# One edge group of the second layer summed in the input projection, and the sum tables zeroed in the first stage

## What is computed

```python
h = relu(layernorm(x)) @ w_in + b_in            # the input projection
for l in range(2):                              # two attention layers
    xn = layernorm(h, ln1_g[l], ln1_b[l])
    q, k, v = xn @ wq[l] + bq[l], xn @ wk[l] + bk[l], xn @ wv[l] + bv[l]
    scores = (q[dst] * k[src]).sum(-1) * scale          # per head, 8 heads
    attn = segment_softmax(scores, dst)
    agg = segment_sum(attn[:, :, None] * v[src], dst)
    h = h + agg @ wo[l] + bo[l]
    h = h + gelu(layernorm(h, ln2_g[l], ln2_b[l]) @ w1[l] + b1[l]) @ w2[l] + b2[l]
x = x + h
h = relu(layernorm(x))
sum3d = segment_sum(edge_attr @ W_sum + b_sum, src)     # needs nothing of the attention layers
x = x + h + z_in[in_deg] + z_out[out_deg] + sigmoid(cent @ W_cent + b_cent) + sigmoid(vor @ W_vor + b_vor) + sum3d
```

## Time and profile before

| | us |
|---|---|
| median of 3 runs | 4973.2 |
| lowest and highest run | 4970.74, 4974.58 |
| span of the profiled execution | 4968.2 |
| PE busy | 3781.3 (76%) |
| DVE busy | 3674.6 (74%) |
| POOL busy | 3293.4 (66%) |
| ACT busy | 2245.8 (45%) |
| costliest line: scatters of the updates, POOL L1523, x600 | 951.8 |

### The profile page before, as it was taken

The page is one execution under the profiler, slowest core; times in us unless marked ns, Lnnn a source line. Parts: engine busy times, 40 slices in busy tenths (PEclk is TensorE's granted clock), DMA queues, the critical chain, the costliest instruction groups (busy, mean ns, idle before and its releaser), DMA issues. The chain is left out here.

```text
span 4968.2 us, 83663 instructions
## 1 busy us (share of the span) xinstructions
PE 3781.3 (76%) x17490; PEld 2898.5 (58%) x17491; DVE 3674.6 (74%) x10004; ACT 2245.8 (45%) x5559; POOL 3293.4 (66%) x2856
## 2 busy tenths in 40 slices
PE   2686677777777776999986677777777776888879
PEld 1344455555555555888853455555555555777766
DVE  5686688888888886666656688888888886666658
ACT  0122455555555553444410455555555563343323
POOL 2266666666666654888877666666666663888866
PEclk9698799988988998999998799999899997999989
DMA  4577666666666655777766666666666654777767
GB/s 107 176 173 172 195 184 180 184 181 180 185 175 184 178 159 127 152 160 153 160 133 132 199 181 187 183 181 181 180 180 181 183 172 97 148 143 148 143 157 222
DMA packets 683884, 831.82 MB, mean 167 GB/s; under 512 B 147301, under 2 KB 524321, under 8 KB 683589
## 3 DMA queue, kind: packets, MB, share of 16 engines
q0 software_dynamic: 261248, 480.06, 40.8%
q1 hardware_dynamic: 389483, 320.59, 22.4%
q10 hardware_dynamic: 32860, 28.05, 1.9%
HBM read 753.81 MB, written 124.16 MB: 177 GB/s over the span
## 5 line engine op out<-in xcount | busy, mean ns | idle before, releaser
L1042 POOL DMA_INDIRECT kv<-kv_scratch,src_u x1760 | 1775.7, 1009 | 955.1 <-issue 532.4
L1308 PE MATMUL sum_p<-msg,hot_s 128*128 128x273 f32 x3520 | 1132.7, 460 | 578.9 <-DVE sums L1174 452.6
L1308 PEld LDWEIGHTS sum_p<-msg,hot_s 128*128 128x128 f32 x3520 | 705.2, 215 | 893.1 <-DVE sums L1174 442.8
L1523 POOL DMA_INDIRECT sum_scratch<-ysum,dest x600 | 951.8, 1586 | 196.8 <-issue 137.8
L1296 PE MATMUL qe<-sums,hot_q 128*128 x3520 | 910.0, 404 | 99.6 <-ACT hot_q L1064 85.7
L1296 PEld LDWEIGHTS qe<-sums,hot_q 128*128 128x128 f32 x3520 | 719.5, 208 | 244.7 <-issue 115.7
L1174 DVE SCALAR_TENSOR_TENSOR sums<-sums,keep,sum_p 128x273 f32 x880 | 433.7, 493 | 463.9 <-remote 402.1
L1073 ACT ACTIVATE hot_s<-iota_f,ndrel_u 128x128 f32<-128x128 f32 x1760 | 558.7, 391 | 223.1 <-remote 173.2
L1148 DVE TENSOR_TENSOR prod<-qe,kv 128x1024 f32<-128x1024 f32 x440 | 535.6, 1217 | 64.2 <-DMA kv<-kv_scratch,src_u 35.0
L1163 DVE TENSOR_TENSOR msg<-kv,turned 128x1024 f32<-128x1024 f32 x440 | 532.6, 1210 | 7.5 <-issue 7.5
L1155 DVE TENSOR_REDUCE S<-prod 128x32 f32<-128x1024 f32 x440 | 533.8, 1213 | 0.6
(11 more groups left out here) (267 smaller groups left out, 5147.8 us busy)
## 6 DMA issues: line engine op xcount, KB each, us to landing
drow<-drel_scratch SPq DMA_DIRECT2D x220, 256.0 KB
kv<-kv_scratch,src_u POOLq DMA_INDIRECT x1760
ea<-in_edge_attr SPq DMA_DIRECT2D x52, 512.0 KB
srow<-in_src_rows SPq DMA_DIRECT2D x52, 512.0 KB
kv_scratch<-res SPq DMA_DIRECT2D x100, 256.0 KB
ea<-in_edge_attr SPq DMA_DIRECT2D x52, 384.0 KB
srow<-in_src_rows SPq DMA_DIRECT2D x52, 384.0 KB
h_scratch<-res SPq DMA_DIRECT2D x150, 128.0 KB
```

What stands on the lines that cost most here:

```text
L1042: g.indirect_dma_start(out=kv[:, slot, :], out_offset=None, in_=KVd, in_offset=bass.IndirectOffsetOnAxis(ap=src_u[:, par, u:u + 1], axis=0 ...
L1308: ins = pe.matmul(sum_p[i][:, 0:XW], hot_s[:, q % 2, 2 * i + u, :], msg[:, q % 2, 2 * i + u, :], start=(u == 0), stop=(u == 1))
L1523: g.indirect_dma_start(out=sum_d[r], out_offset=bass.IndirectOffsetOnAxis(ap=dest[:, k, j:j + 1], axis=0), in_=ysum[:, k, j, :], in_offset ...
```

## The change

It has two parts.

**One more group early.** `OPENING = ((1, 5),)` names layer 1 (the second), group 5. `project(-1)` now handles that group for each of the 50 tiles: two groups a pair (`EN` = 2, `halves` = 1), so one `y_p`, tables 0 and 1 only, one `ysum` copy and two scatters a pair. `OWN = (6, 5)` says how many groups the updates scatter themselves: the second update now has 5 groups a tile, in two parts of 3 and 2, and scatter `j` of tile `k` goes to table `(5k + j) mod 4`. The waits on the four table semaphores in `project(0)` start from the count that `project(-1)` leaves (`scattered(r)`). In `project(-1)` POOL's list gets scales and scatters in turn (`first_turn`), DVE's the compare, the count and the destination of the group, SP's the three loads, and its wait at the end is for the landing of the scatters.

**Zeroing.** The four tables are zeroed in the first stage, on ACT's queue, by 10 stores for each table (semaphore `tables_out`, which POOL waits for before its first scatter), from a tile of zeros `zero`. The 100 stores in `project(-1)` are gone.

```diff
+OWN = (6, 5)
+OPENING = ((1, 5),)
+ZERO_PARTS = 10
+ZERO_W = NT * YW // ZERO_PARTS
...
+                @block.scalar
+                def _(a):
+                    a.wait_ge(zeroed, 1)
+                    for r in range(TABLES):
+                        table = sum_d[r].rearrange("(p a) w -> p (a w)", p=P)
+                        for i in range(ZERO_PARTS):
+                            a.dma_start(table[:, i * ZERO_W:(i + 1) * ZERO_W], zero[:, 0:ZERO_W]).then_inc(tables_out, 16)
...
-            early = l == 0
+            early = l <= 0
+            queries = l == 0
+            EN = 2 * len(OPENING) if first else 2 * HELD
+            halves = EN // 2
...
+                            if first:
+                                for h, (layer, j) in enumerate(OPENING):
+                                    g = layer * NT + t * 2
+                                    sp.dma_start(srow[:, 2 * h * P:(2 * h + 2) * P].rearrange("p (k e) -> p k e", k=2),
+                                                 src_rows[bass.ds(g, 2), j * P:(j + 1) * P].unsqueeze(0).to_broadcast([P, 2, P])
...
-                            if first:
-                                for r in range(TABLES):
-                                    sp.dma_start(sum_d[r][bass.ds(t * 2 * P, 2 * P), :].rearrange("(p a) w -> p (a w)", p=P),
-                                                 sums[:, 0:2 * YW]).then_inc(zero_out, 16)
...
-                        if first:
-                            sp.wait_ge(zero_out, 16 * TABLES * PAIRS)
...
+                        def scale(t, k):
+                            g.wait_ge(ve_s[k], t + 1)
+                            g.tensor_tensor(out=rs[:, k, :], in0=veps[:, k, :], in1=neghalf[:, :],
+                                            op=ALU.pow).then_inc(rs_s[k], 1)
+
+                        def first_turn(t):
+                            scale(t + 1, 1)
+                            if halves == 2 and (not isinstance(t, int) or t > 0):
+                                scatter(t - 1, 1)
+                            scale(t + 2, 0)
+                            scatter(t, 0)
...
+                        if first:
+                            for t, k in ((0, 0), (0, 1), (1, 0)):
+                                scale(t, k)
+                            g.wait_ge(tables_out, 16 * ZERO_PARTS * TABLES)
+                            first_turn(0)
+                            with g.Fori(1, PAIRS) as t:
+                                first_turn(t)
...
                         def early_turn(t):
                             norm(t + 1, 0)
+                            if first:
+                                stats(t + 1, 1)
                             results(t, 0)
...
                             compare(t)
                             norm(t + 1, 1)
+                            if first:
+                                stats(t + 2, 0)
                             results(t, 1)
                             repeats(t)
                             destination(t, 0)
...
-                groups = EG if held is not None else EG - HELD
-                PARTS = ((0, 0, 3), (1, 3, EG - HELD), (0, EG - HELD, EG))[0:3 if held is not None else 2]
+                own_n = OWN[l]
+                groups = own_n + HELD if held is not None else own_n
+                PARTS = ((0, 0, 3), (1, 3, own_n), (0, own_n, own_n + HELD))[0:3 if held is not None else 2]
```

More of the change, by code:

```diff
@@ L500, in wait, with scattered @@
                         eng.wait_ge(sem, v)
+                def scattered(r):
+                    return 0 if first or r >= 2 * len(OPENING) else 16 * PAIRS
                 def scatters_done(eng, t, h):
                     for r in (2 * h, 2 * h + 1):
-                        wait(eng, early_s[r], t * 16)
+                        wait(eng, early_s[r], t * 16 + scattered(r))
                 with nc.Block() as block:
@@ L653, in _ @@
                                             base=0, pattern=[[-1, P]], channel_multiplier=1).then_inc(tril_s, 1)
+                        if first:
[5 more added lines that the diff above has]
+                                first_turn(t)
+                            if halves == 2:
+                                scatter(PAIRS - 1, 1)
+                            for r in range(EN):
+                                g.wait_ge(early_s[r], 16 * PAIRS)
+                        elif early:
                             for h in range(2):
@@ L799, in early_turn @@
                             destination(t, 0)
-                        if not first:
+                        if first:
+                            for k in range(2):
+                                stats(0, k)
+                        else:
                             v.wait_ge(scales_s, 1)
-                            for k in range(2):
-                                norm(0, k)
+                        for k in range(2):
+                            norm(0, k)
+                        if first:
+                            stats(1, 0)
                         if early:
@@ L867, in sum_groups @@
                         def sum_groups(t):
-                            pe.wait_ge(ea_in, t * 32 + 32)
+                            pe.wait_ge(ea_in, (t + 1) * 16 * halves)
                             pe.wait_ge(same_s, t * ES + 2)
-                            for h in range(2):
+                            for h in range(halves):
                                 wait(pe, y_ev[h], t)
@@ L1420, in scatters @@
                     return sum(table(k, j, n) == r for j in range(n))
-                own_n = EG - HELD
                 def part(t, k, b, j0):
                     n = t * 2 + k
-                    return n * 2 + j0 // (EG - HELD) if b == 0 and held is not None else n
+                    return n * 2 + j0 // own_n if b == 0 and held is not None else n
                 per = [[16 * scatters(k, r, own_n) for r in range(TABLES)] for k in range(2)]
-                sc0 = [[l * 16 * scatters(k, r, EG - HELD) * PAIRS for r in range(TABLES)] for k in range(2)]
+                sc0 = [[sum(16 * scatters(k, r, OWN[i]) * PAIRS for i in range(l)) for r in range(TABLES)] for k in range(2)]
                 S3N = groups + 5
@@ L1509, in scatter @@
                             for b, j0, j1 in PARTS:
-                                if held is not None and j0 == EG - HELD:
+                                if held is not None and j0 == own_n:
                                     continue
```

83 lines of the change are left out of this document (38 added, 45 removed).

## The result

The changed kernel takes 4987.1 us in the median of 7 runs (4981.39 to 4995.88), the kernel before 4970.7 us in 7 runs on the same chip. The ratio is 1.0029, with a 95% interval of 1.0017 to 1.0042: slower by 0.29%, a small loss, with 1 outside the interval. The forecast was 4985, slower. The profiled execution of the changed kernel has a span of 4988.5 us against 4968.2. One later execution of the changed kernel, in which the chip granted 0.56 of TensorE's clock instead of 0.90, took 6109 us; it stands in no median and no ratio of this text.

The account below looks back on a forecast made before the run. POOL was taken to bound the second update, a DVE chain the first projection. From 4968.2 us, +73 + 10.7 + 6 + 2 - 79, less about 1, gave 4980; the runs' median being 5.0 above the profile, 4985 us, range 4948 to 5010.

Parts of the forecast that it names:

- The second update: Second update: one scatter a tile fewer saves 88.8 us with POOL as the bound, less 10: a gain of 79 us.
- the landing wait: Second update: an even tile's first scatter waits for an earlier landing on table 0, 0.4 us a pair, 10 us lost (0 to 38).
- that rival: Second update: PE becomes the bound if its clock falls below 1.00, costing up to 79 us; within the rest, chance 0.08.
- The first projection's loop: First projection: a pair of tiles takes 8.7 instead of 5.74 us, +73 us (52 to 86).
- count from the end of dest: First projection: along POOL's queue after dest, scatters start at 0.89 and 2.74 us, rs and xn come at 4.93.
- The first rival: First projection: DVE does not wait for rs, 52 instead of 73 us, 4964; chance 0.24, shared with no landing wait.
- The rival at 7.8 a pair: First projection: the no-scale-wait rival, a pair at 7.8 us if only DVE counts; chance 0.24, shared with no landing wait.
- The end of the stage: End of first projection: two last scatters must land and POOL drain, 13.2 us against 2.5 now, +10.7 us.
- The zeroing: First stage: 40 stores on ACT delay the stage's own stores and barrier, +6 us (0 to 17).
- The rival's sign: First stage: ACT cannot issue its 40 stores before 45 us, so zeroing holds up the start; up to 17 us, 4996, chance 0.12.
- The Trainium skill's rule of turns: First stage: queues alternate packet by packet, so the moved zeroing would cost next to nothing, 6 us less than taken.
- The Trainium skill's port rule: First projection: scatters and DVE block each other, each stretched by one xn, 20 us, 5005; within the rest, chance 0.08.

## Why the prediction was right, step by step

- **The second update.** Right in sign, size and mechanism: 88.8 less 10 for the landing wait. Measured 85.3: the time from the first to the last `rs` fell by 77.8, where 79 was forecast, and the rest is gained ahead of the first `rs` (3.1) and behind the last (4.3), of which the prediction had only 1. The wait for the landing was there, 0.5 us a pair where 0.4 was put. Tiles at 10.2 us were forecast and measured. That PE would be the next in line, with 0.1 us to spare, the 97 of 100 us confirm, and the run with the other table order, which came to 9.92 us a tile. PE's granted clock stayed at 1.00 there, so that rival did not come.
- **The first projection's loop.** Forecast 8.7 us a pair, measured 8.77. Its parts were less exact than their sum: DVE alone needs 7.56, not 7.8 (the run without scatters), and the wait for `rs` is 1.05, not 0.8. The path through POOL was exact: 0.91, 2.80 and 4.97 us after `dest`, against 0.89, 2.74 and 4.93. The step "count from the end of dest" is why the two errors cancel: the pair was summed along POOL's path, where DVE's own list doesn't enter. Of the +2 us for the new loads ahead of the weights some 0.6 shows: the first `xn` comes 12.6 us after the start of the stage instead of 12.0.
- **The first rival** (no wait for the scale) did not come, and its price of 21 us stays untested. The run that took the wait away gave 3.3 us. It did so by putting `rs` between the scatters, and this made the ring over the landing, `ysum` and the next scatter longer, to 8.63 us. The prediction has this ring: ACT's `ysum` "needs the landing of the turn before, 2.74 + 4.9 = 7.6, and ends at 8.1, before the dest at 8.7, so it hides". It hides at 8.7. The rival at 7.8 a pair didn't carry it on; with the scatters 1.89 us apart, the ring of 7.7 us (estimated above) would just have hidden there too.
- **The end of the stage.** +10.7 forecast, +9.0 measured in the changed kernel: 8.7 us from the last scatter's start to the next work and not the 10.5 of the earlier trace rows.
- **The zeroing.** The one term that was off by half: +6 taken, +12.9 measured, inside the bounds of 0 to 17. The step that failed is "the stage's own packets are small and share the engines in turn", taken as a reason for a small price. They did share in turn, 442 packets of either queue from 49 to 52 us, and being small is what hurt: 0.11 MB against 1.04. Besides, their first packet moved 3.8 us after the issue instead of 0.9, and the two guards needed 5.29 us of issue instead of 1.46; the runs don't show why. The next stage began 12.3 us after the issue of the last store instead of 4.5, and some 5 us after the end of the zeroing. The rival's sign did not come: ACT, which before issues nothing in this stage, had issued its 40 stores by 44.0 us, and nothing of the stage waits for their landing. The price stands near the rival's all the same, by way of SP's stores and the gathers.
- **The Trainium skill's rule of turns.** The Trainium skill, "DMA: Bandwidth & Descriptors", section "Queues, rings and completion order", says that an engine goes round the queues packet by packet. The trace agrees, as far as packets are counted. What did not follow from it is the prediction's "lose at most a packet's time each": a transfer is many packets (the stage's last stores are 2116 in all), and each of them can stand behind one of the zeroing's. With "next to nothing" for the zeroing the forecast would have been 4979, and a little worse.
- **What the sum owes to luck.** The zeroing was put 7 us too low, the gain of the update 5 us too low, and the projection 2 us too high; the three stages add up to 12.9 + 83.5 - 85.3 = +11.1, and +11.7 was forecast. So errors of 7, 5 and 2 us cancelled. The medians differ by 16.4 and the ratio on the other chip says 16 as well, so some 5 us more lie in stages that the forecast put at zero. A candidate is the second projection: 247.3 to 248.3 us in four profiles without scatters in the first projection, 248.0 to 251.9 in the eight with them. But the changed kernel itself gave 249.8 and 248.0, so it isn't settled. Against the median of 7 runs the base of 4973.2 was 2.5 us high, which took the forecast as much nearer to the 4987.1.
- **The Trainium skill's port rule** ("SBUF — State Buffer", "SBUF: two separate sides") gave a rival of 20 us, one `xn` of 0.41 us for each scatter. That section has the lock for DVE instructions in a 2-port mode or with two inputs in SBUF; no trace here shows an instruction's mode. The prediction's row against it was misread: that `xn` ends at 348.62, and the scatter begins at 348.60. In the first projection of the changed kernel `xn` is over at 205.62 and the scatter starts at 205.69, so it tells nothing either. The run with two buffers does have them together: scatters with an `xn` beside them take 1.60 to 1.67 us there (16 of them), the others behind an `rs` 1.59 (17). That is at most 0.1 us and not 0.41, so the rule's price does not show. What became longer beside POOL's work in the changed kernel is the two `same`, by 0.05 us a pair, 1 us over the stage; in the rows of the run with two buffers they take 0.48 us, as without scatters.

## What to carry to other kernels

Before work is moved into a stage that looks idle, follow every ring that it closes (issue, landing, buffer, next issue) and write its length beside the length of the turn, for the repair too: here the ring of 7.7 us grew to 8.63 with the repair, which gave 3.3 of 26 us until the ring was broken as well. A free share of the DMA engines is not free bandwidth: read the GB/s beside it. And compare the size of the packets of two queues that meet: of two that take turns, the one with the small packets gets the small part of the bytes, and if it stands at the end of the stage, the stage waits. And a moved piece of work costs its landing once more at the end of the stage that takes it, here 8.6 us for two scatters.

## What was not expected of the hardware

Between 18 and 23 us the DMA engines are busy and move almost nothing, in both kernels. Windows rows, first of the changed kernel, then of before:

```profile
18.00:23.00 5.00, 0.00 (x0) 0.00 (x0) 0.00 (x0) 0.00 (x0) 3.78 (x5) 1.00 0.76 25
...
28.00:40.00 12.00, 0.00 (x0) 0.00 (x0) 4.69 (x11) 0.00 (x0) 2.07 (x3) 1.00 1.05 391
```

```profile
18.00:23.00 5.00, 0.00 (x0) 0.00 (x0) 0.00 (x0) 0.00 (x0) 3.78 (x5) 1.00 0.78 31
```

At a share of 0.76 the changed kernel moves 25 GB/s while the same zeroing moves 391 a few microseconds later. The stretch is behind a store of single 4-byte elements (`nt_scratch`, issued at 13.4) and has the first gathers under way. By queue (18 to 23 us, before and changed; `q0` carries the gathers) the share is of few and slow packets:

```profile
q0 software_dynamic: 71, 0.16, 78.1%
...
q10 hardware_dynamic: 44, 0.10, 65.1%
```

Before, these are the gathers' own packets, 0.9 us each; in the changed kernel the zeroing's packets are as slow, 1.2 us each, where they take 0.1 later. The 4-byte packets of the store are through by 18 us, 900 of them in the 5 us before; whether the store's after-effect or the gathers slow the rest wasn't tried. The zeroing moves 0.66 MB from 18 to 28 us, worth 1.7 us at 391 GB/s: an estimate of 8 us lost. The prediction had counted the free share of this stretch, like that of the whole stage, as room for the zeroing.

The second surprise is small: `rs`, a 128x1 operation of 0.55 us, takes 1.15 to 1.3 us in the rows where it follows a scatter directly: it is shown as starting before the scatter has ended, and ends 0.6 us behind it. On POOL an operation behind a scatter is best counted from the scatter's end.
